# A graph layer's mean on one core: VectorE's transposes one chunk ahead in its opening, the second tile asked for sooner, and a tail with the root's table loaded early and two logarithms on ScalarE

## The reference

```
h = max(layernorm(x), 0)
x = x + attention(h, adj, ...)            # layer 0
h = max(layernorm(x), 0)
X = mobius_matvec(W, h)                   # points; artanh and tanh of their norms
gamma = 2 / (1 - |X|^2)
mean  = (adj @ (gamma X)) / (adj @ (gamma - 1))
mean  = mean / (1 + sqrt(1 - |mean|^2))
alpha = row sums of adj
y = tanh(alpha * artanh(|mean|)) * mean / |mean|
y = expmap0(relu(logmap0(y)))
x = x + y
```

## Time and profile before

| | us |
|---|---|
| median of 3 runs (803.08 to 804.35) | 803.59 |
| the profiled execution's own time | 802.18 |
| its span, first to last instruction | 800.4 |
| TensorE busy | 741.1 (93%) |
| VectorE busy | 641.1 (80%) |
| ScalarE busy | 480.4 (60%) |
| GpSimd busy | 101.3 (13%) |
| mean granted TensorE clock | 0.978 of full |

### The profile page before, as it was taken

The page is one execution under the profiler, slowest core; times in us unless marked ns, Lnnn a source line. Parts: engine busy times, 40 slices in busy tenths (PEclk is TensorE's granted clock), DMA queues, the critical chain, the costliest instruction groups (busy, mean ns, idle before and its releaser), DMA issues.

```text
span 800.4 us, 14756 instructions
## 1 busy us (share of the span) xinstructions
PE 741.1 (93%) x4989; PEld 684.7 (86%) x4996; DVE 641.1 (80%) x1238; ACT 480.4 (60%) x876; POOL 101.3 (13%) x212
## 2 busy tenths in 40 slices
PE   4999989999999999998978799999999999999980
PEld 4888768788888888887878699999999999999980
DVE  6878576777787778888787779888888888888874
ACT  3444366777777789777852555555544555555753
POOL 0000111221111222167000000000000000000080
PEclk9999989999999999999999999999999999999995
DMA  5116377677777766778907598999998998889541
GB/s 145 54 53 237 115 267 289 250 250 281 291 289 285 261 239 239 275 250 184 219 21 158 129 208 185 201 202 199 190 219 190 189 188 190 190 191 197 123 159 56
DMA packets 53000, 157.26 MB, mean 196 GB/s; under 512 B 8656, under 2 KB 30416, under 8 KB 46800
## 3 DMA queue, kind: packets, MB, share of 16 engines
q1 hardware_dynamic: 52944, 156.60, 71.6%
HBM read 148.16 MB, written 8.42 MB: 196 GB/s over the span
## 4 chain that ended last, share of the span: by engine, by line
PE 43%; issue 28%; DVE 10%; POOLq 5%; DMA 5%; ACT 4%; DVEq 2%; POOL 1%; SPq 1%; ACTq 0%
PE bank L673 42%; DMA adjL<-in_adj 3%; DVE adjT_lo L1515 3%; ACT adjT_hi L1015 2%; POOLq L599 1%; DVE bank L1507 1%; POOLq L619 1%; DVE turned L1507 1%; POOLq L605 1%; PE bank L665 1%; POOLq L549 1%; POOL q_low L557 1%; DMA w_raw<-in_L_gnn_Wv 1%; DVE X_lo L1495 1%; POOLq L603 1%
## 5 line engine op out<-in xcount | busy, mean ns | idle before, releaser
L673 PE MATMUL bank<-X_hi,adjT_hi 128*128 128x258 f32 x1024 | 292.2, 285 | 18.2 <-DVE adjT_lo L1515 18.2
L673 PE MATMUL bank<-X_lo,adjT_hi 128*128 128x258 f32 x1024 | 291.0, 284 | 0.0
L673 PE MATMUL bank<-X_hi,adjT_lo 128*128 128x258 f32 x1024 | 290.3, 284 | 0.0
L673 PEld LDWEIGHTS bank<-X_hi,adjT_hi 128*128 128x128 f32 x1024 | 194.5, 190 | 21.6 <-DVE adjT_lo L1515 17.2
L673 PEld LDWEIGHTS bank<-X_lo,adjT_hi 128*128 128x128 f32 x1024 | 195.0, 190 | 0.0
L673 PEld LDWEIGHTS bank<-X_hi,adjT_lo 128*128 128x128 f32 x1024 | 194.9, 190 | 0.0
L819 PE MATMUL bank<-values,probT 128*128 128x256 f32 x512 | 120.7, 380 | 1.2 <-ACT probT L1133 1.2
L1015 ACT CAST adjT_hi<-turned 128x1024 fp32r<-128x1024 f32 x64 | 67.1, 1048 | 70.6 <-PE bank L673 54.5
L1015 ACT CAST adjT_hi<-bank 128x1024 fp32r<-128x1024 f32 x64 | 64.8, 1013 | 68.9 <-PE bank L673 44.1
L819 PEld LDWEIGHTS bank<-values,probT 128*128 128x128 f32 x512 | 93.0, 190 | 14.2 <-ACT probT L1133 2.1
L1515 DVE TENSOR_TENSOR adjT_lo<-bank,adjT_hi 128x1024 fp32r<-128x1024 f32 x64 | 77.2, 1207 | 18.4 <-ACT adjT_hi L1015 18.3
(11 more groups left out here) (191 smaller groups left out, 1121.7 us busy)
## 6 DMA issues: line engine op xcount, KB each, us to landing
adjL<-in_adj SPq DMA_DIRECT2D x120, 512.0 KB, 8.5
adjU<-in_adj SPq DMA_DIRECT2D x32, 1024.0 KB, 7.8
adjL<-in_adj SPq DMA_DIRECT2D x16, 2048.0 KB, 7.8
x_scratch<-x SPq DMA_DIRECT2D x16, 258.0 KB, 3.1
xin<-in_x SPq DMA_DIRECT2D x8, 512.0 KB, 3.9
xt<-in_x SPq DMA_DIRECT2D x16, 256.0 KB, 6.6
adj<-in_adj SPq DMA_DIRECT2D x8, 512.0 KB, 16.0
x_all<-x_scratch SPq DMA_DIRECT2D x16, 256.0 KB, 10.6
```

The costliest lines, as they stand in the source:

```text
L673: last = pe.matmul(dst, a[i][a_cols], b[j][b_cols], start=(k_first and n == 0), stop=(k_last and n == 2))
```

## The change

**Opening, VectorE.** The transposes move ahead by one instruction: from chunk 7 on, the transpose of chunk n + 1 stands before the low part of chunk n, and the scales of tiles 0 and 1, made together before, are made one at a time, the first after the low part of chunk 14 and the second after that of chunk 15. The rows are of VectorE from the transpose of chunk 15 on (`turned_3` and `bank12` hold turned chunks, `adjT_lo3` chunk 15 before; `sgn` to `turn` are the scales). Before:

The two logarithms take away VectorE's work on the quotient (two additions, a reciprocal, a product); the choice between series and logarithm is now made by multiplying alpha with 0 or 1 in two instructions. The diff, cut to its core:

```diff
-FINISH_FUNCTIONS = [(ACT.Sqrt, "squares", "roots"), (ACT.Ln, 5, 5), (ACT.Tanh, 1, 3)]
+FINISH_FUNCTIONS = [(ACT.Sqrt, "squares", "roots"), (ACT.Ln, 2, (4, 5)), (ACT.Tanh, 1, 3)]
...
                         mean_adj(0, first_adj[0], d_adj[0])
+                        x_pair(s)
+                        sp.wait_ge(s_expB, HT)
+                        sp.wait_ge(s_qk_used, (HC + 1) * (HT - 1) + HC)
+                        mean_adj(1, first_adj[1], d_adj_1)
...
                 steps(sp, step)
-                sp.wait_ge(s_expB, HT)
-                sp.wait_ge(s_qk_used, (HC + 1) * (HT - 1) + HC)
-                mean_adj(1, first_adj[1], d_adj_1)
                 norms_back(PAIRS - 2, PAIRS - 1)
...
-                        points_whole(EARLY_PIECES[BEFORE_LAST:])
+                        points_whole(EARLY_PIECES[BEFORE_LAST:-4])
+                    if is_step(s, HT - 1):
+                        points_whole(EARLY_PIECES[-4:])
...
+                    elif fn == ACT.Ln:
+                        act.activation(v[dst[0]][:, cols], v[src][:, cols], fn, bias=ones[:, 0:1])
+                        act.activation(v[dst[1]][:, cols], v[src][:, cols], fn, scale=-1.0,
+                                       bias=ones[:, 0:1]).then_inc(s_fa, 1)
...
                 points_high(6)
+                adj_high(9)
                 points_high(7)
-                for n in range(9, FIRST):
+                for n in range(10, FIRST):
                     adj_high(n)
                     if n > 12:
                         mean_out(n - 13, (n - 13) % 2)
-                for t in range(2):
-                    mean_squares(t, t, 2)
+                    if n > 13:
+                        mean_squares(n - 14, n - 14, n - 13)
...
                 mean_squares(T - 2, 0, T - 1)
+                act.activation(junk[:, 2, 0:1], ones[:, 0:1], ACT.Sqrt)
                 mean_out(T - 1, 1)
...
-                    ts(V[2][:, c], V[1][:, c], EPS, CLIP, ALU.max, ALU.min)
+                    ts(V[2][:, c], V[1][:, c], EPS, CLIP, ALU.max, ALU.min).then_inc(s_f, 1)
                     ts(V[1][:, c], V[1][:, c], EPS, None, ALU.max)
-                    dve.drain()
-                    artanh_start(V[2][:, c], V[5][:, c], V[6][:, c])
...
+                first_turn(7)
                 adj_low(6)
                 points_edge(1)
-                first_turn(7)
                 points_low(4)
+                first_turn(8)
                 adj_low(7)
                 points_low(5)
-                first_turn(8)
+                first_turn(9)
                 adj_low(8)
-                first_turn(9)
                 points_low(6)
+                first_turn(10)
                 adj_low(9)
                 points_low(7)
-                for n in range(10, FIRST):
+                for n in range(11, FIRST):
                     first_turn(n)
-                    adj_low(n)
+                    adj_low(n - 1)
+                    if n == FIRST - 1:
+                        mean_scales(0, 1, 1)
                 adj_turn(4, 0, 0, FIRST)
-                mean_scales(0, 2, 2)
+                adj_low(FIRST - 1)
+                mean_scales(1, 1, 2)
```

More of the change, by code:

```diff
@@ L464, in step @@
                         sp.dma_start(adjU[:, 0:HALF], adj_t[nxt.tile(HALFWAY) + HT][:, 0:HALF]).then_inc(s_beside, 16)
-                    x_pair(s)
+                        x_pair(s)
                     if s.par == 0 and after(s, 3):
@@ L1350, in tt @@
                 return dve.tensor_tensor(o, a, b, op)
-            def artanh_start(a, t1, t2):
-                ts(t1, a, -1.0, 1.0, ALU.mult, ALU.add)
-                ts(t2, a, 1.0, None, ALU.add)
-                dve.drain()
-                dve.reciprocal(t1, t1)
-                dve.drain()
-                tt(t1, t1, t2, ALU.mult).then_inc(s_f, 1)
             def artanh_series(a, t2, t3):
@@ L1370, in artanh_series @@
                 dve.scalar_tensor_tensor(out=t3, in0=t3, scalar=1.0, in1=a, op0=ALU.add, op1=ALU.mult)
[L1371 to L1381, removed]
             V = [a[:, :] for a in v]
@@ L1548, in finish_series @@
                     dve.reciprocal(V[1][:, c], V[1][:, c])
+                    dve.scalar_tensor_tensor(out=V[8][:, c], in0=V[2][:, c], scalar=TINY_ARG, in1=alpha[:, c], op0=ALU.is_lt,
+                                             op1=ALU.mult)
                     dve.drain()
+                    dve.scalar_tensor_tensor(out=V[6][:, c], in0=V[2][:, c], scalar=TINY_ARG, in1=alpha[:, c],
+                                             op0=ALU.is_ge, op1=ALU.mult)
                     tt(V[0][:, c], V[0][:, c], V[1][:, c], ALU.mult)
+                    tt(V[7][:, c], V[7][:, c], V[8][:, c], ALU.mult)
                 def finish_scaled(c):
-                    artanh_end(V[2][:, c], V[5][:, c], V[6][:, c], V[7][:, c])
-                    tt(V[2][:, c], V[2][:, c], alpha[:, c], ALU.mult)
+                    dve.drain()
+                    function_done()
+                    tt(V[2][:, c], V[4][:, c], V[5][:, c], ALU.subtract)
+                    dve.drain()
+                    dve.scalar_tensor_tensor(out=V[2][:, c], in0=V[2][:, c], scalar=0.5, in1=V[6][:, c], op0=ALU.mult,
+                                             op1=ALU.mult)
+                    dve.drain()
+                    tt(V[2][:, c], V[2][:, c], V[7][:, c], ALU.add)
                     dve.drain()
```

## The result

| | before | after |
|---|---|---|
| median, us (runs) | 803.34 (4, 802.92 to 804.35) | 795.71 (4, 793.98 to 796.69) |
| the profiled execution's own time | 802.18 | 796.11 |
| its span | 800.4 | 794.3 |

The ratio is 0.9902, with a 95% interval of 0.9882 to 0.9921: faster by 7.6 us, one per cent. The forecast was 796.8, with a range of 793.0 to 800.5. The one profile of after began 0.68 us late: a store that stood at 349.56 us before stands at 350.24, ahead of all that the change touches. I call this the shift of a profile (the start of its store less 349.56) and take it off where times from the start of the span are compared between kernels.

What follows compares the result with a forecast made beforehand. TensorE's 2232 matmuls were taken to bound the kernel, so gains had to come ahead or behind. Terms -6.8 + 0.8 - 0.8 + 0.05 = -6.75 put the profiled 802.18 at 795.4, the median at 796.8 us; range 793.0 to 800.5.

Steps and rivals of the forecast that it cites:

- d, tile 2: Opening: how much later tile 2 lands for VectorE; taken as +0.8 us, ends -3.4 and +3.
- new order in the opening: Chunk 6 to chunk 16: VectorE's waits for casts go and chunk 16 starts sooner; -6.8 us, ends 0 and -9.4.
- finish of 24 tiles: Finish of the first 24 tiles: ScalarE's logarithm no longer waits for VectorE's quotient; -0.8 us, ends -0.9 and 0.
- load: Tail, ScalarE: early load and one-column root cost +1.5 us on the path, a later load goes, -0.75; net +0.75.
- logarithms, tail: Tail: VectorE's series starts sooner, less two more products and a wait; net -0.7 us, ends 0 and -1.
- Tile 1 sooner: Opening, SyncE: tile 1 requested ahead of the store, which queues behind it and delays tile 2's request; gains nothing, +0.8 us.
- GpSimd's pieces: zero: Opening: four pieces later remove TensorE's 2.02 us wait for the masking, hidden by VectorE's wait for tile 2; zero.
- Tail: End of the kernel: the load's +0.75 and the logarithms' -0.7 us together, +0.05.
- The clock at chunk 16: TensorE's clock after 2.6 us idle: a fall taken as likelier; rival, it stays up, 795.3 us, chance 0.29.
- The rivals on the queue: Opening: store overtakes tile 1, 792.6 us, chance 0.04; or store takes 19.6 us and holds SyncE, 806.0, chance 0.06.
- The rival of half the gain: Opening: tile 4 later, or ScalarE holding cast 16 as before, leaves half the new order's term; 800.2 us, chance 0.06.

Runs made afterwards that it cites:

- e3: The kernel before with only the opening's new order on VectorE and ScalarE: 795.49 us, ratio 0.9902.
- e2: The kernel before with only SyncE's new order, tile 1 asked for ahead of the store: 803.55 us, ratio 1.0002.
- e9: The changed kernel with GpSimd's last four pieces ahead of the last masking again: 795.87 us, ratio 0.9913.
- e6: The changed kernel with VectorE's quotient and one logarithm again, in both finishes: 796.13 us, ratio 0.991.
- e1: The changed kernel with SyncE's order of before, the store ahead of tile 1's transfers: 795.29 us, ratio 0.9896.
- e8: The changed kernel with tile 2 asked for ahead of reading back the norms: 792.01 us, ratio 0.9867.
- e4: The changed kernel without the root of one column (the early table load) in the tail: 794.4 us, ratio 0.9894.
- e5: The changed kernel with the root of one column moved ahead of the squares of tile 30: 793.58 us, ratio 0.9881.
- e11: The changed kernel with each load of x1 asked for ahead of its pair of adj tiles: 791.53 us, ratio 0.9864.

## Why the prediction was right, and where its sizes were off

By the profiles, after less before, term by term (they sum to -6.0; the spans differ by 794.3 - 800.4 = -6.1). Without the shift that is -6.7, almost the -6.75 of the forecast, but this closeness is luck: the new order gave 0.6 more than its term, and tile 2 took 0.7 more than its own.

| term | predicted | measured, us | from |
|---|---|---|---|
| the shift, ahead of the change | none | +0.7 | the store at 349.56 and 350.24 |
| d, tile 2 | +0.8 | +1.5 | 393.57 - 392.04 |
| new order in the opening | -6.8 | -7.4 | 42.01 - 49.44 |
| finish of 24 tiles | -0.8 | -0.7 | 326.11 - 326.79 |
| load | +0.75 | +0.7 | 1.48 - 0.80 |
| logarithms, tail | -0.7 | -0.8 | 5.62 - 6.44 |

- *What bounds.* Right: only the work ahead of the 2232 matmuls and behind them counted, and these did not change.
- *The new order.* Right, and shown alone by e3. Chunk 10 came 22.0 us behind the transpose of chunk 6 (22.3 by the working), TensorE set the pace from there, and there was no wait ahead of chunk 15. The squares of one tile took 1.74 (437.20 to 438.94; 1.8 taken). The 0.6 us by which the term was small are such tenths: chunk 16 stands 42.0 behind chunk 6, not 42.6.
- *Tile 1 sooner.* The mechanism was right (without the shift the store landed at 378.2, 378.4 predicted; tile 2 was asked for at 380.1, 380.6 predicted; nothing gained), the attribution of d was not. SyncE's order by itself is +0.16 (e2); the +1.2 that the working gave is not there, since tile 2 was asked for 0.6 us sooner than worked out (380.02) and landed 12.2 us later instead of 12.6. The rest of the +1.5 goes with GpSimd's pieces.
- *GpSimd's pieces: zero.* The step that failed. That the 2.0 are hidden is shown by e9. But something else goes with their place: tile 2 is about 1.5 us later with them behind the masking, in all seven profiles, and the prediction had no term for it. Its likely cause, a packet of code ahead of tile 2's last quarter (e9), is not shown. The medians are too coarse to show these 1.5 us (e9 has 795.87, after 795.71).
- *Finish.* TensorE's idle time went from 0.86 to 0.27, not to zero: 0.6 of the 0.8. e6 brings it back.
- *Tail.* The load is on the path at +1.5 and takes 0.8 off behind; the logarithms give 0.8.
- *The clock at chunk 16.* The case of a fall was taken as likelier, the other had 0.29. Both happen. With the same idle time ahead of chunk 16 (TensorE is busy for 0.13 to 0.17 us of the last 2.6) the clock fell in five profiles (after, e1, e3, e8, e9) and stayed in four (e4, e5, e6, e11); here one stretch of each, e8's and e5's:

```profile
442.38:445.88 3.50, 3.50 (x18) 3.50 (x19) 3.50 (x4) 1.13 (x2) 0.00 (x0) 0.56 0.02 5
```

```profile
446.80:450.30 3.50, 3.50 (x29) 3.50 (x30) 3.50 (x4) 1.13 (x2) 0.00 (x0) 1.00 0.03 5
```

  It is worth 1.3 to 1.5 us (269.1 to 269.3 against 267.8 for the 2232 matmuls). So a kernel that stops here may have two times; that this is a part of the 2.7 us by which after's runs differ is likely, but only one of them was profiled.
- *The rivals on the queue.* The store didn't overtake tile 1, and it wasn't held for 19.6 us but for 10.70. The Trainium skill ("DMA: Bandwidth & Descriptors", section "Queues, rings and completion order") allows a later transfer to be done first; in this trace it was not: the store landed behind tile 1.
- *The rival of half the gain.* Neither of its causes came: the transpose of chunk 16, the first that needs tile 4, starts at 437.08 with no idle time before it, and the cast of chunk 16 was not held as long as before.

## What to carry to other kernels

Where one engine makes what the next one consumes, put the producer's work one item ahead and ask of each instruction on the slower engine what stands behind it: here the order of a few instructions gave 7.4 us, and the request made sooner gave nothing. An earlier request on a queue that serves in order, as the store behind tile 1 was served here, moves the wait to whatever is queued behind it, so the next wait on that queue is to be found before the gain is counted. And price work that is "off the path" by what it does to its neighbours: 18 us of additions on GpSimd, which no list of waits names, cost 3 us here by making many of VectorE's small operations up to four times as long.

## What the runs showed of the hardware that was not expected

- VectorE's operations on one or two columns are 0.15 to 0.17 us long, and most of them 0.45 to 0.7 while GpSimd adds tiles of 128x256 in 0.73 us each (e11 against after). The Trainium skill ("SBUF — State Buffer", section "SBUF: two separate sides") says that VectorE, in an operation of a mode that uses two ports or with two inputs in SBUF, shares one pair of ports with GpSimd, which the first to start holds for its whole instruction. The trace agrees in this: the long ones last nearly as long as one addition, and they are short once the additions are not beside them. Which of the operations are of such a mode it doesn't show, and a few beside the additions stay short.
- The granted clock after nearly the same idle time, 2.44 to 2.47 us, fell in five profiles out of nine; what decides it is not shown.
- The DMA view counts packets of instructions on the same 16 engines as the data. One of 16 KB, 1.2 to 1.4 us long, starts at 390.6 to 393.0 us (without the shift) in each of the eleven profiles compared above, and by the times it makes the last quarter of tile 2 (after) or the first of tile 3 (e9) land some 1.3 us or more later. That is read from profiles alone, and no run tests it.
